# Bias products of an attention block as rows instead of columns, and the preparation of the MLP weights one slot earlier

## The chip, the cores and the metric

The kernel runs on one core of a Trainium2 chip. The metric is the device time of one execution in microseconds. TensorE does the matrix products, VectorE, ScalarE and GpSimd (POOL) the elementwise work, and SyncE (SP) issues all DMAs. TensorE's clock has two levels, 1.2 and 2.4 GHz; the profile gives the granted one as 0.50 and 1.00.

## The reference, cut to what matters

One block of cross attention with an MLP, for 16 batches of 256 queries and 256 tokens, width 512, 16 heads of 32, hidden width 2048:

```
q, kv = ln(x) * g_q + b_q, ln(ctx) * g_kv + b_kv
qp, kp, vp = q @ Wq.T + bq, kv @ Wk.T + bk, kv @ Wv.T + bv
scores = qp . kp / sqrt(32) - scale * dist + offset      # per head
x = x + softmax(scores) @ vp @ Wo.T + bo
h = gelu((ln(x) * g_m + b_m) @ W1.T + b1)
out = x + h @ W2.T + b2
```

The layer norms' shifts b_q, b_kv and b_m are not added to the activations. As (y * g + b) @ W.T is y @ (g * W).T + b @ W.T, the gains go into the weights and the products b @ W.T (the "shifts' products") into the biases. The change is about those products.

## The kernel before, in words

All large products are f16 in three passes (high by high, high by low, low by high), so each weight is split once into a rounded high part and the rest. Before that it is scaled by the inverse of a norm: ScalarE squares the staged f32 weight and sums over its rows, VectorE adds up, TensorE sums over partitions (`total`), VectorE copies the sum and works out the square of the norm (`square_norm`), GpSimd takes the root (`norm_root`), VectorE forms the factor (`gains`), ScalarE writes the high part (`weight_hi`, `w1_hi`, `w2_hi`) and VectorE the low part (`weight_lo`, `w1_lo`, `w2_lo`). W1 and W2 are staged in 8 chunks of 4 pieces (128x512) in a ring of three chunks. W2's split pieces are stored to DRAM (`store_w2`), since only three fit on the chip, and are loaded again for every batch (`load_w2`).

Each engine has its own program, an order written out by hand over the same slots, from -32 to 297. One slot is one item: one head of one batch. In slot s TensorE computes the scores of item s+1 (`scores`, one bank of PSUM, so it waits until VectorE has read the scores before), VectorE takes the maximum of item s (`score_max`, line 1054), ScalarE the exponentials (`exps`, line 773), and so on down the pipeline. Projections of queries and keys come every four slots, those of values and outputs every sixteen. `mlp_up` starts in slot 31 and `mlp_down` in slot 37 (`DOWN`); from there each slot holds one step of each. Slots -32 to -1 prepare the attention weights, slots 1 to 35 those of the MLP, beside the attention's first items. Within an engine all runs in order, so a waiting instruction holds everything behind it.

`weight_bias`, `value_bias` and `w1_bias` make the shifts' products: the weight's 128x128 f32 block is the loaded operand, one column of `cols` the moving one, so the result is a column of 128. There are 16 such products for each of W_k, W_q, W_v and each chunk of W1; each appears as two records of `128x1 f32`. `bias_column`, `bias_v_spread` and `bias1_columns` read the columns from PSUM. `value_bias_out` (line 541) multiplies W_v's bias, spread over a tile, by W_o. `warm` (line 653) and `keep_busy` (line 659) are fillers: products whose result nobody reads. `keep_busy` runs in slots 7 to 36 and fills each slot to 16 units of one 512 column product.

Of the kernel before, what the change touches and what calls it, by code (L numbers as in the profile page):

```python
# [13 lines left out]
P = 128  # L14
# [37 lines left out]
def build_block(nc, x, ctx, tok_xy, q_xy, mask, w_qkv, w_o, w_1, w_2, cols, b_o, b_2, sp_scale, sp_offset, out, w2_dram):  # L52
# [16 lines left out]
    with es:  # L69
# [80 lines left out]
        sq = sb("sq", [P, LC, T], F32, at["x1_n"])  # L150
        bias_v = sb("bias_v", [P, KT, P], F32, at["x1"] + KT * D * 4)
# [51 lines left out]
        s_mkept, s_tv, s_brow, s_bcol, s_brow_o, s_bo_all = sem("s_mkept"), sem("s_tv"), sem("s_brow"), sem("s_bcol"), sem("s_brow_o"), sem("s_bo_all")  # L203

# [18 lines left out]
        TOTAL = (-30, -28, -4, 0) + tuple(range(1, 33, 4))  # L223
        NORM = (-28, -25, -3, 0) + tuple(range(2, 34, 4))
        GAIN = (-27, -24, -3, 1) + tuple(range(3, 35, 4))
# [122 lines left out]
        def sync_program(engine):  # L348
# [49 lines left out]
            def load_residual(t):  # L398
                ring = t % X1_RING
                gate.wait_ge(s_wsq, WSQ[3])  # L400
                gate.wait_ge(s_brow_o, 1)
                gate.wait_ge(s_mkept, DMA)
                gate.wait_ge(s_colsum, 1)
                gate.wait_ge(s_store[ring], DMA * (t // X1_RING))
                e.dma_start(x1[:, ring, :], x_rows[t]).then_inc(s_res[ring], DMA)
# [43 lines left out]
            for slot in range(FIRST_SLOT, LAST_SLOT + 1):  # L449
# [42 lines left out]
                for step in due(slot, -5, ITEM, 2 * N_CHUNKS * KT):  # L492
# [5 lines left out]
        def tensor_program(engine):  # L498
            e, gate = engine, Gate(engine)

            def weight_bias(sec, quarters):
# [3 lines left out]
                for k in quarters:  # L505
                    gate.wait_ge((s_wk if sec == SEC_K else s_wq)[k], DMA)
                    for m in range(KT):

                        col = sec * KT + m
                        mm = e.matmul(ps_bias[sec][:, col:col + 1], w_stage[sec][:, k, m * P:(m + 1) * P],  # L510
                                      cols_sb[:, b_ln + k:b_ln + k + 1], start=((k, m) == (0, 0)), stop=((k, m) == (KT - 1, KT - 1)))
                if KT - 1 in quarters:
                    mm.then_inc(s_brow)

            def value_bias(m):
                sec, b_ln = SEC_V, B_KV
                gate.wait_ge(s_w[0], DMA)
                gate.wait_ge(s_cols, DMA)
                gate.wait_ge(s_bcol, BIAS_Q)
                col = sec * KT + m  # L520
                for k in range(KT):
                    mm = e.matmul(ps_bias[sec][:, col:col + 1], w_stage[sec][:, k, m * P:(m + 1) * P],
                                  cols_sb[:, b_ln + k:b_ln + k + 1], start=(k == 0), stop=(k == KT - 1))
                if m == KT - 1:
                    mm.then_inc(s_brow)

            def w1_bias(c, m):
                col = c * CH + m
                for k in range(KT):
                    gate.wait_ge(s_wc[c % C_STAGES][k], n_staged(c))  # L530
                    mm = e.matmul(ps_bias_1[:, col:col + 1], staged(c, k)[:, m * P:(m + 1) * P],
                                  cols_sb[:, B_M + k:B_M + k + 1], start=(k == 0), stop=(k == KT - 1))
                if m == CH - 1:
# [114 lines left out]

            def warm(count):
# [15 lines left out]
            for slot in range(FIRST_SLOT, LAST_SLOT + 1):  # L665
                for at_slot, count in ((-32, 10), (-30, 3), (-8, 10), (-6, 8), (-3, 2), (-2, 8)):
# [42 lines left out]
        def scalar_program(engine):  # L709
# [72 lines left out]
            def dist_square(b, c):  # L782
# [4 lines left out]
                gate.wait_ge(s_hlo, 2 * (b - 2))  # L787
# [583 lines left out]
```

## Time and profile before

| | us |
|---|---|
| median of 3 runs (1252.31 to 1252.36) | 1252.32 |
| the profiled execution | 1252.47 |
| its span, first to last instruction | 1250.6 |
| TensorE busy | 1220.2 |
| VectorE busy | 993.6 |
| GpSimd busy | 992.0 |
| ScalarE busy | 851.3 |
| mean granted clock of TensorE | 0.986 |

Busy times are of the span, whatever the stage. A group of instructions is named by line, engine, operation and tiles (out, then in). In the order of time several equal instructions are merged, with their count behind an x. The idle time in brackets is the engine's own before the instruction, with the one that ended it.

### The profile page before, as it was taken

How to read it: one execution, taken by the hardware profiler on the slowest of the kernel's cores; microseconds unless marked ns; L12 is line 12 of the kernel's file. 1: busy time of each engine (PE TensorE's matmuls, PEld its weight loads, DVE VectorE, ACT ScalarE, POOL GpSimd, SP SyncE). 2: the span in 40 equal slices, each digit the busy share in tenths (PEclk: the TensorE clock that was granted, in tenths of full speed). 3: DMA queues.
4: the chain of work that ended last, by engine and by line, in shares of the span. 5: the costliest groups of instructions: out<-in, count | busy, mean ns of one | idle time of the engine just before them, and what ended most of it. 6: DMA issues, size and time to landing. Idle time of an engine off the chain costs nothing.

```text
span 1250.6 us, 27744 instructions
## 1 busy us (share of the span) xinstructions
PE 1220.2 (98%) x9424; PEld 819.0 (65%) x9424; DVE 993.6 (79%) x2656; ACT 851.3 (68%) x1914; POOL 992.0 (79%) x1286
## 2 busy tenths in 40 slices
PE   9888988999999999999999999999999999999998
PEld 6656455666667666666666676666666666666664
DVE  5799998888878888888888989888888787778321
ACT  5867757676877677676767677776767677676331
POOL 5478897989898898989898998989898987767320
PEclk9788999999999999999999999999999999999999
DMA  6699999888999898998999998998889897879543
GB/s 185 197 188 208 224 224 195 192 189 209 209 194 222 180 214 198 193 203 201 198 205 218 180 223 182 202 203 203 194 206 208 195 208 176 173 170 180 142 113 123
DMA packets 468686, 241.69 MB, mean 193 GB/s; under 512 B 384048, under 2 KB 408896, under 8 KB 468544
## 3 DMA queue, kind: packets, MB, share of 16 engines
q1 hardware_dynamic: 468544, 239.91, 85.6%
q8 instruction: 75, 1.23, 0.4%
q14 instruction: 67, 0.55, 0.1%
HBM read 109.66 MB, written 12.58 MB: 98 GB/s over the span
## 4 chain that ended last, share of the span: by engine, by line
PE 86%; DVE 8%; issue 2%; ACT 1%; POOL 1%; DMA 1%; SPq 0%; POOLq 0%; DVEq 0%; ACTq 0%
PE ps_up L630 26%; PE ps_down L645 26%; PE ps_qk L566 12%; PE ps_vo L590 6%; PE ps_vo L587 6%; PE ps_s L601 5%; PE ps_pv L615 4%; DVE p_nat L1071 1%; DVE soft L1054 1%; PE ps_down L510 1%; DVE w L999 1%; DVE w L1005 1%; DVE x_nat L1031 1%; PE ps_down L541 0%; DVE qk_parts L1045 0%
## 5 line engine op out<-in xcount | busy, mean ns | idle before, releaser
L1248 POOL TENSOR_SCALAR p_nat<-soft,row_inv 128x256 f16<-128x256 f32 x512 | 332.1, 658 | 61.2 <-DVE row_inv L1065 59.4
L630 PE MATMUL ps_up<-hT,w 128*128 128x256 f16 x3072 | 377.2, 273 | 3.1 <-ACT u L805 2.7
L645 PE MATMUL ps_down<-w,hid 128*128 128x512 f16 x1536 | 372.9, 379 | 0.8 <-DVE hid L1103 0.4
L630 PEld LDWEIGHTS ps_up<-hT,w 128*128 128x128 f16 x3072 | 300.3, 98 | 93.2 <-ACT u L805 3.2
L773 ACT ACTIVATE soft<-soft,neg_max 128x256 f32<-128x256 f32 x512 | 255.2, 500 | 117.2 <-DVE neg_max L1054 116.2
L1054 DVE CUSTOM_DVE_ANT_0 soft<-ps_s,soft,factor 128x256 f32<-128x256 f32 x512 | 225.4, 476 | 116.7 <-PE ps_s L601 115.9
L1071 DVE SCALAR_TENSOR_TENSOR p_nat<-soft,row_inv,p_nat 128x256 f16<-128x256 f32 x512 | 297.6, 620 | 2.1 <-POOL p_nat L1248 1.9
L1256 POOL TENSOR_SCALAR soft<-dist,scale_neg,offset 128x512 f32<-128x512 f32 x256 | 244.3, 954 | 14.0 <-DVE p_nat L1071 13.6
L645 PEld LDWEIGHTS ps_down<-w,hid 128*128 128x128 f16 x1536 | 148.6, 97 | 132.4 <-DMA w<-x_scratch 1.4
L805 ACT ACTIVATE u<-ps_up,bias,up_scale 128x256 f32<-128x256 f32 x256 | 142.3, 556 | 124.9 <-PE ps_up L630 121.5
L1264 POOL TENSOR_SCALAR hid<-u,hid_scale 128x1024 f16<-128x1024 f32 x64 | 77.3, 1208 | 105.0 <-ACT u L811 105.0
L766 ACT ACTIVATE qk_parts<-ps_qk,bias_qkv 128x512 f16<-128x512 f32 x128 | 86.9, 679 | 100.1 <-DMA stack<-stack 83.3
L1103 DVE SCALAR_TENSOR_TENSOR hid<-u,hid_scale,hid 128x1024 f16<-128x1024 f32 x64 | 98.0, 1531 | 47.9 <-POOL hid L1264 47.9
L601 PE MATMUL ps_s<-stack 97*128 97x256 f16 x512 | 100.6, 278 | 17.4 <-DVE neg_max L1054 17.0
L566 PE MATMUL ps_qk<-xT,w_q 128*128 128x256 f16 x768 | 99.2, 281 | 2.6 <-DVE qk_parts L1045 2.6
L566 PE MATMUL ps_qk<-xT,w_k 128*128 128x256 f16 x768 | 96.2, 276 | 0.7 <-DVE qk_parts L1045 0.7
L773 ACT ACTIVATION_READ_ACCUMULATOR soft<-soft,neg_max 128x1 f32 x512 | 96.5, 188 | 0.0
L587 PE MATMUL ps_vo<-w_v,xT 128*128 128x512 f16 x384 | 95.8, 387 | 0.0
L590 PE MATMUL ps_vo<-w_o,attnT 128*128 128x512 f16 x384 | 93.3, 379 | 0.0
L566 PEld LDWEIGHTS ps_qk<-xT,w_q 128*128 128x128 f16 x768 | 77.2, 101 | 14.2 <-issue 1.7
L566 PEld LDWEIGHTS ps_qk<-xT,w_k 128*128 128x128 f16 x768 | 76.1, 99 | 11.7 <-DVE qk_parts L1045 1.4
L601 PEld LDWEIGHTS ps_s<-stack 97*128 97x128 f16 x512 | 44.5, 99 | 58.3 <-issue 28.3
(122 smaller groups left out, 1569.5 us busy)
## 6 DMA issues: line engine op xcount, KB each, us to landing
w<-x_scratch SPq DMA_DIRECT2D x256, 256.0 KB, 3.1
stack<-qk_parts SPq DMA_DIRECT2D x256, 96.0 KB
raw<-in_ctx SPq DMA_DIRECT2D x32, 256.0 KB, 3.4
raw<-in_x SPq DMA_DIRECT2D x32, 256.0 KB, 3.1
c_stage<-in_w SPq DMA_DIRECT2D x32, 256.0 KB, 3.6
x<-in_x SPq DMA_DIRECT2D x32, 256.0 KB, 3.5
out<-x SPq DMA_DIRECT2D x32, 256.0 KB, 3.2
tok_rows<-in_tok_xy SPq DMA_DIRECT2D x16, 256.0 KB, 4.4
```

The source lines that it names most:

```text
L566: mm = e.matmul(ps_qk[:, which * L:(which + 1) * L], w_sec[sec][:, wp, k, hg * P:(hg + 1) * P], xT_of(b, which)[:, :, xp * KT + k, :], sta ...
L587: mm = e.matmul(ps_vo[:], xT_of(b, 0)[:, tt, xp * KT + k, :], w_sec[SEC_V][:, wp, k, :], start=first, stop=last)
L590: mm = e.matmul(ps_vo[:], attnT[:, b % 2, xp, k, tt * P:(tt + 1) * P], w_sec[SEC_O][:, wp, k, :], start=first, stop=last)
L601: mm = e.matmul(ps_s[:, lc * T:(lc + 1) * T], stack[0:97, ring, j, 0, lc * P:(lc + 1) * P], stack[0:97, ring, j, 1, :], start=True, stop=True)
L630: mm = e.matmul(ps_up[s % 2][:, 0:L], w_1_sb[:, wp, k, m * P:(m + 1) * P], hT[:, b % 2, :, xp * KT + k, :], start=(k, wp, xp) == (0, 0, 0) ...
L645: mm = e.matmul(ps_down[tt][:], hid[:, chunk % HID_RING, i, hp, tt * P:(tt + 1) * P], w_2_sb[:, s % W2_RING, wp, :], start=(m == 0 and (hp ...
L773: e.activation(soft[:, ring, lc, :], soft[:, ring, lc, :], ACT.Exp, scale=-1.0, bias=neg_max[:, ring, lc:lc + 1], accum_out=row_sum[:, rin ...
L805: e.activation(u[:, chunk % U_RING, i, :], ps_up[s % 2][:, 0:L], ACT.Identity, scale=up_scale[:, chunk % N_CHUNKS:chunk % N_CHUNKS + 1], b ...
L1054: e.tensor_tensor_reduce(soft[:, ring, lc, :], ps_s[:, lc * T:(lc + 1) * T], soft[:, ring, lc, :], factor[:, 0:1], 3.0e38, ALU.add, ALU.mi ...
L1071: mine = e.scalar_tensor_tensor(out=p_nat[:, nat, LO, lc, :], in0=soft[:, ring, lc, :], scalar=row_inv[:, ring, lc:lc + 1], in1=p_nat[:, n ...
L1248: mine = e.tensor_scalar(p_nat[:, nat, HI, lc, :], soft[:, ring, lc, :], row_inv[:, ring, lc:lc + 1], 1.0, ALU.mult, ALU.mult)
L1256: e.tensor_scalar(soft[:, i % SOFT_RING, :, :], dist[:, b % DIST_RING, :, :], scale_neg[:, h:h + 1], offset_sb[:, h:h + 1], ALU.mult, ALU. ...
```

## The change

The shift's column becomes the loaded operand (one column) and the weight the moving one, 512 f32 columns at a time, read in the order "every 128th column first". The result is one row, in which four values of one partition lie side by side. ScalarE copies the row to on-chip memory (`bias_row`, `bias_rows_1`) and a DMA on SP's queue turns it into columns (`bias_turn`, `bias_turn_1`); W1's four rows lie on partitions 0, 32, 64 and 96 of one bank, which a filler product clears first (`clear_rows`). The squares of distances wait for the turned row of W_q, whose place they use. W_v's product moves from slots -2, 0 and 2 to slot -3. Chunk loads, squares, totals, gains, roundings and stores of W1 and W2 move one slot ahead, and with them the hidden norm; W2's piece 0 is loaded in slot 35 instead of 36, the others as before. `keep_busy` starts in slot 0 instead of 7, into another bank up to slot 8, and counts a product of W1 as 4 units instead of 8. The fillers ahead of the first slots are regrouped.

```diff
-        TOTAL = (-30, -28, -4, 0) + tuple(range(1, 33, 4))
-        NORM = (-28, -25, -3, 0) + tuple(range(2, 34, 4))
-        GAIN = (-27, -24, -3, 1) + tuple(range(3, 35, 4))
+        TOTAL = (-30, -28, -4, 0) + tuple(range(0, 32, 4))
+        NORM = (-28, -25, -3, 0) + tuple(range(1, 33, 4))
+        GAIN = (-27, -24, -3, 1) + tuple(range(2, 34, 4))
...
+            def bias_turn(sec):
+                gate.wait_ge(s_row, AT[sec] + 1)
+                e.dma_start(bias_qkv[:, sec * KT:(sec + 1) * KT], (row_q if sec == SEC_Q else row_kv)[:]).then_inc(s_rowd[sec], DMA)
+
+            def bias_turn_1():
+                gate.wait_ge(s_row, ROW_1)
+                for c in range(N_CHUNKS):
+                    e.dma_start(bias_1[:, c * CH:(c + 1) * CH], rows_1[32 * c:32 * c + 1, :]).then_inc(s_rowd_1, DMA)
...
+                for sec, at_slot in ((SEC_K, -25), (SEC_Q, -24), (SEC_V, -1)):
+                    if slot == at_slot:
+                        bias_turn(sec)
+                if slot == 18:
+                    bias_turn_1()
...
-                for s in due(slot, 21, ITEM, MT):
+                for s in due(slot, 20, ITEM, MT):
                     store_w2(s)
-                if slot == DOWN - 1:
-                    load_w2(0)
-                for s in due(slot, DOWN - 1, ITEM, N_STEPS - 1):
-                    load_w2(s + 1)
+                for s in due(slot, DOWN - 2, ITEM, N_STEPS):
+                    load_w2(s)
...
-                for step in due(slot, -5, ITEM, 2 * N_CHUNKS * KT):
+                for step in due(slot, -6, ITEM, 2 * N_CHUNKS * KT):
                     load_chunk(*divmod(step, KT))
...
+            def by_column(w):
+                return w.rearrange("p (m q) -> p q m", m=KT)
...
                 for k in range(KT):
-                    mm = e.matmul(ps_bias[sec][:, col:col + 1], w_stage[sec][:, k, m * P:(m + 1) * P],
-                                  cols_sb[:, b_ln + k:b_ln + k + 1], start=(k == 0), stop=(k == KT - 1))
...
+                    mm = e.matmul(ps_bias[sec][0:1, :], cols_sb[:, b_ln + k:b_ln + k + 1], by_column(w_stage[sec][:, k, :]),
+                                  start=(k == 0), stop=(k == KT - 1))
+                mm.then_inc(s_brow)
+
+            def w1_bias(c, k):
+                gate.wait_ge(s_wc[c % C_STAGES][k], n_staged(c))
+                mm = e.matmul(ps_bias_1[32 * c:32 * c + 1, :], cols_sb[:, B_M + k:B_M + k + 1], by_column(staged(c, k)),
+                              start=(k == 0), stop=(k == KT - 1))
...
-                for at_slot, count in ((-32, 10), (-30, 3), (-8, 10), (-6, 8), (-3, 2), (-2, 8)):
+                for at_slot, count in ((-32, 10), (-30, 1), (-28, 1), (-8, 12), (-6, 6)):
...
-                for sec, quarters, at_slot in ((SEC_K, range(3), -31), (SEC_K, range(3, KT), -29), (SEC_Q, range(1), -29),
-                                              (SEC_Q, range(1, 3), -28), (SEC_Q, range(3, KT), -27)):
+                for sec, at_slot in ((SEC_K, -31), (SEC_Q, -29), (SEC_V, -3)):
                     if slot == at_slot:
-                        weight_bias(sec, quarters)
-                for m, at_slot in enumerate((-2, 0, 2, 2)):
-                    if slot == at_slot:
-                        value_bias(m)
+                        weight_bias(sec)
+                if slot == 0:
+                    clear_rows()
...
-                if 7 <= slot < DOWN:
+                if 0 <= slot < DOWN:
                     taken = 1 + (3 if due(slot, 9, GROUP, N_HG) else 0) + (6 if slot % 2 else 0) + (6 if slot >= UP else 0)
-                    taken += vo_done + (8 if due(slot, 1, ITEM, MT) else 0)
-                    keep_busy(max(0, SLOT_STEPS - taken))
+                    taken += vo_done + (4 if due(slot, 1, ITEM, MT) else 0)
+                    taken += 16 if slot == 4 else 0
+                    keep_busy(ps_pv if slot < 9 else ps_down[0], max(0, SLOT_STEPS - taken))
...
+            def bias_row(sec):
+                gate.wait_ge(s_brow, AT[sec] + 1)
+                if sec == SEC_V:
+                    gate.wait_ge(s_rowd[SEC_K], DMA)
+                e.activation((row_q if sec == SEC_Q else row_kv)[:], ps_bias[sec][0:1, :], ACT.Copy).then_inc(s_row)
@@ dist_square
                 gate.wait_ge(s_hlo, 2 * (b - 2))
+                gate.wait_ge(s_rowd[SEC_Q], DMA)
...
+                for sec, at_slot in ((SEC_K, -26), (SEC_Q, -24), (SEC_V, -2)):
+                    if slot == at_slot:
+                        bias_row(sec)
+                if slot == 17:
+                    bias_rows_1()
...
-                for step in due(slot, -3, ITEM, 2 * N_CHUNKS * KT):
+                for step in due(slot, -4, ITEM, 2 * N_CHUNKS * KT):
                     chunk_square(*divmod(step, KT))
-                for step in due(slot, 3, ITEM, MT):
+                for step in due(slot, 2, ITEM, MT):
                     w1_hi(*divmod(step, KT))
-                for s in due(slot, 19, ITEM, MT):
+                for s in due(slot, 18, ITEM, MT):
                     w2_hi(s)
...
-                for n in due(slot, 1, KT, 2 * N_CHUNKS):
+                for n in due(slot, 0, KT, 2 * N_CHUNKS):
                     weight_sums(AT_W1 + n)
...
-                for step in due(slot, 4, ITEM, MT):
+                for step in due(slot, 3, ITEM, MT):
                     w1_lo(*divmod(step, KT))
-                for s in due(slot, 20, ITEM, MT):
+                for s in due(slot, 19, ITEM, MT):
                     w2_lo(s)
```

## Rows read from the trace of the kernel before

**Rows 1.** The page: the chain that ended last, by engine.

```profile
PE 86%; DVE 8%; issue 2%; ACT 1%; POOL 1%; DMA 1%; SPq 0%; POOLq 0%; DVEq 0%; ACTq 0%
```

**Rows 2.** Busy time of PE, PEld, DVE, ACT, POOL; PEclk; last row line 1054 alone.

```profile
39.80:49.50 9.70, 9.48 (x52) 7.04 (x52) 5.40 (x21) 9.49 (x23) 2.82 (x4) 0.65 0.69 212
78.40:115.60 37.20, 30.30 (x232) 22.44 (x232) 36.48 (x112) 29.68 (x79) 30.96 (x42) 0.87 0.97 227
115.60:198.00 82.40, 75.47 (x553) 44.42 (x552) 77.44 (x232) 55.90 (x146) 68.58 (x92) 0.98 0.93 212
210.00:1145.00 935.00, 934.99 (x7522) 632.93 (x7520) 783.23 (x2083) 671.32 (x1500) 811.68 (x1047) 1.00 0.91 198
...
78.40:115.60 37.20, 7.96 (x36) 0.87 0.97 227
```

**Rows 3.** The same columns, for stretches of one clock.

```profile
41.10:47.90 6.80, 6.80 (x29) 4.58 (x28) 3.12 (x14) 6.59 (x19) 2.82 (x4) 0.50 0.68 204
51.40:54.80 3.40, 2.61 (x25) 2.53 (x23) 3.26 (x11) 2.28 (x5) 2.40 (x5) 1.00 0.87 318
54.80:65.00 10.20, 9.30 (x30) 5.82 (x31) 9.96 (x33) 5.95 (x18) 9.71 (x15) 0.50 0.36 85
```

**Rows 4.** TensorE in order of time, 0 to 20 us.

```profile
1.52 4.45 PE L653 MATMUL ps_pv<-attnT 128*128 128x512 f16 x10 [1.52 <-POOL attnT L1283]
6.17 5.25 PE L510 MATMUL ps_down<-cols,w_stage 128*128 128x1 f32 x24 [0.21 <-DMA w_stage<-in_w_qkv]
12.81 6.96 PE L510 MATMUL ps_down<-cols,w_stage 128*128 128x1 f32 x32
19.63 0.57 PE L552 MATMUL ps_up<-sums,one 128*128 128x2 f32 x2
```

**Rows 5.** TensorE in order of time, three places.

```profile
51.28 1.84 PE L522 MATMUL ps_down<-cols,w_stage 128*128 128x1 f32 x16
...
60.59 5.80 PE L541 MATMUL ps_down<-w_stage,bias_v 128*128 128x512 f32 x8
...
189.70 2.10 PE L659 MATMUL ps_down<-w_k 128*128 128x512 f16 x9
```

**Rows 6.** VectorE in order of time: the copies of W_q's and W_o's totals.

```profile
20.24 0.16 DVE L889 COPY tot<-ps_up 128x2 f32<-128x2 f32 x1 [2.98 <-PE ps_up L552]
...
44.14 0.16 DVE L889 COPY tot<-ps_up 128x1 f32<-128x1 f32 x1 [3.37 <-PE ps_up L552]
```

**Rows 7.** ScalarE in order of time, 24 to 52 us.

```profile
24.64 2.56 ACT L740 ACTIVATE w_q<-w_stage,gain 128x512 f16<-128x512 f32 x4 [5.12 <-DVE factor L919]
...
35.70 2.56 ACT L740 ACTIVATE w_v<-w_stage,gain 128x512 f16<-128x512 f32 x4 [0.41 <-DVE gain L913]
38.17 0.58 ACT L734 ACTIVATE ps_down<-c_stage 128x512 f32<-128x512 f32 x1
...
51.26 0.60 ACT L757 ACTIVATE v_parts<-ps_vo 128x512 f16<-128x512 f32 x1
```

**Rows 8.** Waits, 38 to 210 us: total, times, longest.

```profile
PE ps_s L601 <- DVE neg_max L1054: 17.0, 15, 2.8
DVE row_one L1062 <- ACT soft L773: 3.6, 1, 3.6
DVE b_o L979 <- PE ps_down L541: 1.2, 1, 1.2
DVE v_parts L1040 <- ACT v_parts L757: 0.9, 2, 0.7
```

**Rows 9.** ScalarE and TensorE in order of time, at the first gelu.

```profile
194.54 0.72 ACT L752 ACTIVATE w<-c_stage,w_scale 128x512 f16<-128x512 f32 x1 [1.64 <-DMA x_scratch<-w]
...
202.49 1.48 PE L630 MATMUL ps_up<-hT,w 128*128 128x256 f16 x12 [2.75 <-ACT u L805]
```

**Rows 10.** DMA issues up to 230 us: size, us from issue to landing.

```profile
stack<-mask_row SPq DMA_DIRECT2D x1, 8.0 KB, 2.3
...
q_neg<-in_q_xy SPq DMA_DIRECT2D x1, 32.0 KB, 5.0
```

More of the change, by code:

```diff
@@ L401, in load_residual @@
                 gate.wait_ge(s_brow_o, 1)
-                gate.wait_ge(s_mkept, DMA)
-                gate.wait_ge(s_colsum, 1)
+                if t >= KT:
+                    gate.wait_ge(s_rowd_1, N_CHUNKS * DMA)
                 gate.wait_ge(s_store[ring], DMA * (t // X1_RING))
@@ L499, in tensor_program, with weight_bias @@
             e, gate = engine, Gate(engine)
-            def weight_bias(sec, quarters):
+            def by_column(w):
+                return w.rearrange("p (m q) -> p q m", m=KT)
+            def weight_bias(sec):
                 gate.wait_ge(s_cols, DMA)
                 b_ln = B_Q if sec == SEC_Q else B_KV
[L505 to L509, printed above, removed]
-                        mm = e.matmul(ps_bias[sec][:, col:col + 1], w_stage[sec][:, k, m * P:(m + 1) * P],
-                                      cols_sb[:, b_ln + k:b_ln + k + 1], start=((k, m) == (0, 0)), stop=((k, m) == (KT - 1, KT - 1)))
-                if KT - 1 in quarters:
-                    mm.then_inc(s_brow)
@@ L527, in w1_bias @@
[L527 to L533, printed above, removed]
+                if sec == SEC_V:
+                    gate.wait_ge(s_row, ROW_K)
+                for k in range(KT):
+                    if sec == SEC_V:
+                        gate.wait_ge(s_w[0], DMA)
+                    else:
+                        gate.wait_ge((s_wk if sec == SEC_K else s_wq)[k], DMA)
+                    mm = e.matmul(ps_bias[sec][0:1, :], cols_sb[:, b_ln + k:b_ln + k + 1], by_column(w_stage[sec][:, k, :]),
+                                  start=(k == 0), stop=(k == KT - 1))
@@ L647, in mlp_down, with clear_rows @@
                 mm.then_inc(s_m2)
+            def clear_rows():
+                e.matmul(ps_bias_1[:], w_sec[SEC_K][:, HI, 0, 0:P], w_sec[SEC_K][:, HI, 0, :], start=True, stop=True)
             def warm(count):
@@ L653, in warm, with keep_busy @@
                     e.matmul(ps_pv[:], fill[:, 0, 0:P], fill, start=True, stop=True)
-            def keep_busy(count):
-                gate.wait_ge(s_bo_all, 1)
+            def keep_busy(bank, count):
+                if bank is ps_down[0]:
+                    gate.wait_ge(s_bo_all, 1)
+                gate.wait_ge(s_wlo, AT[SEC_K] + 1)
                 for _ in range(count):
-                    e.matmul(ps_down[0][:], w_sec[SEC_K][:, HI, 0, 0:P], w_sec[SEC_K][:, HI, 0, :], start=True, stop=True)
+                    e.matmul(bank[:], w_sec[SEC_K][:, HI, 0, 0:P], w_sec[SEC_K][:, HI, 0, :], start=True, stop=True)
             STEPS = KT * len(PASSES)
@@ L960, in bias_column @@
                 part = slice(sec * KT, (sec + 1) * KT)
-                gate.wait_ge(s_brow, AT[sec] + 1)
-                e.tensor_tensor(bias_qkv[:, part], ps_bias[sec][:, part], cols_sb[:, B_IN + sec * KT:B_IN + (sec + 1) * KT], ALU.add).then_inc(s_bcol)
+                gate.wait_ge(s_rowd[sec], DMA)
+                e.tensor_tensor(bias_qkv[:, part], bias_qkv[:, part], cols_sb[:, B_IN + sec * KT:B_IN + (sec + 1) * KT], ALU.add).then_inc(s_bcol)
                 gate.wait_ge(s_bcol, 2 * AT[sec] + 1)
@@ L967, in bias_v_spread @@
             def bias_v_spread():
-                gate.wait_ge(s_brow, AT[SEC_V] + 1)
+                gate.wait_ge(s_rowd[SEC_V], DMA)
                 gate.wait_ge(s_wsq, WSQ[3])
                 part = slice(SEC_V * KT, (SEC_V + 1) * KT)
-                e.tensor_tensor(bias_qkv[:, part], ps_bias[SEC_V][:, part], cols_sb[:, B_IN + SEC_V * KT:B_IN + (SEC_V + 1) * KT],
+                e.tensor_tensor(bias_qkv[:, part], bias_qkv[:, part], cols_sb[:, B_IN + SEC_V * KT:B_IN + (SEC_V + 1) * KT],
                                 ALU.add).then_inc(s_tv)
@@ L1133, in vector_program @@
                         gains(w)
-                if slot == 32:
+                if slot == 31:
                     hidden_norm()
-                if slot == 34:
+                if slot == 33:
                     hidden_scales()
@@ L1149, in vector_program @@
                     bias_out()
-                if slot == 19:
+                if slot == 21:
                     bias1_columns()
@@ L1290, in gpsimd_program @@
                         norm_root(w)
-                if slot == 33:
+                if slot == 32:
                     norm_root(N_W)
```

27 lines of the change are left out of this document (15 added, 12 removed).

## The prediction

> **What bounds the kernel now.** I read the chain of waits first, then the table of stretches, then the clock, then the order of time in the first 210 us. The chain gives 86% to TensorE [rows 1]. The table by stage says more. From 210 to 1145 us TensorE is busy 934.99 of 935 us at full clock [rows 2]; nothing of the change issues there (W2's loads for steps 1 and up keep their slots), so that stage is a constant, and only the moment at which it begins can move. Before it the bound is another. From 78.4 to 115.6 us VectorE is busy 36.48 of 37.20 us for 9 items (line 1054 has 36 records there, four per item), so 4.13 us an item; from 115.6 to 198 it is 77.44 of 82.40. TensorE has 30.30 and 75.47 there [rows 2], and in 38 to 210 us it waits 17.0 us, 15 times, for VectorE to read the score bank [rows 8]. From 39.8 to 49.5 us it is ScalarE, busy 9.49 of 9.70 us, where VectorE has 5.40 [rows 2]. Before that nothing is full: one chain of small results runs from W_q's products to W_v's rounding.
>
> The clock is low in places, and not where TensorE rests. Between 51.4 and 54.8 us TensorE is busy 2.61 of 3.40 us, nearly all of it 128x1 products, and the next 10.2 us are granted 0.50, which is 1.2 GHz; so are 41.1 to 47.9 us, after another set of them [rows 3, 5]. The page of the skill that bears on it says otherwise (below).
>
> **The change, part by part.** My unit is the profiled execution, 1252.47 us (span 1250.6 and 1.87 around it); the median of the runs is 0.15 lower.
>
> *Products of W_k and W_q.* Before: 16 products each of 128 columns loaded for one moved. 32 records took 6.96 us [rows 4], so 16 products take 7.0 us at 1.2 GHz. W_k's run from 6.17 us, and W_q's total stands at 19.63 us behind 56 records, 5.25 + 6.96 us [rows 4]. After: 4 products each with 512 f32 columns moved. The one group of that size took 5.80 us for 4, part of it at 0.50 [rows 3, 5]; its records are pairs, so each product is four passes over 512 columns. A pass is about 0.21 us at 2.4 GHz (nine f16 ones end in 2.10 us, the last 0.38 included) and 0.43 us at 1.2 GHz (ten in 4.45 us) [rows 4, 5]. So 0.86 or 1.71 us a product, 3.4 or 6.8 us a matrix. If the clock rises once wide columns stream without a pause, W_k's products end between 10 and 12 us, W_q's total would be free at 14 to 16 us, and ScalarE's sums of squares and VectorE's first W_k rounding, ahead of it on their queues, hold it near 16. VectorE waited 2.98 us for this total [rows 6], and behind it ScalarE 5.12 us for W_q's factor [rows 7]; all work up to W_v's gain at 35.7 us hangs on it. That is 3.6 us at most by this one wait, and I take 3.0, since W_q's row must now turn before ScalarE may square the distances. That wait is new: row copy 0.6 us, then a small DMA. The nearest landings are 2.3 us (mask row) and 5.0 us (coordinates) [rows 10]; at 2.3 it ends inside ScalarE's idle 5.12 us, at 5.0 it gives back about 2 us. On SP's queue nothing is due behind it but the turns of the query tiles, which are not ready. If the clock stays low, 2 x 6.8 us and three small groups end at 20.9: 1.3 later than now. Bounds -4.5 and +1.3; I take **-3.0**.
>
> *W_v's product, in slot -3.* It leaves slots -2 to 2 (four times eight records, of which sixteen take 1.84 us at full clock; [rows 5]) and puts 3.4 us, or 6.8 cold, ahead of the second key projection. TensorE had fillers and idle time there, and the copy of its row stands behind ScalarE's own queue. 0; at 6.8 us the first scores come late by up to 3, still before ScalarE takes them up.
>
> *ScalarE before the first exponentials.* This is what the change costs. The squares of a W1 chunk move one slot ahead, so one more stands in front (0.58 us, and 0.2 as my estimate for the read of its sum), and the copy of W_v's row is new, 128x512 before for about 0.60 us [rows 7]; its bounds are 0.25 and 0.67, 0.60 is the nearest row. The other copies fall into idle time. From W_v's rounding at 35.70 us to 50 us ScalarE has no room [rows 2, 7]: 1.4 us. Worse, W1's first total now stands in slot 0 beside W_o's: VectorE sums chunk 0 before it takes W_o's total, and TensorE's queue (value projection, next scores) stands behind W1's total. Today VectorE waits 3.37 us for W_o's total until 44.14 [rows 6]; TensorE would free it some 1.5 us sooner, without eight narrow records at half clock, but ScalarE gives the square later, so nothing is won, and about 0.5 is lost. **+1.9**, bounds +0.6 and +3.
>
> *Slots 0 to 17.* A W1 step is one product of 0.86 us where eight records take 0.95 (16 in 1.84; [rows 5]). By the formula fillers go from 167 to 239: 36 in slots 0 to 6, and up to 4 more (0.86 us) in each of slots 7 to 16. A slot is then filled to about 16 x 0.215 = 3.5 to 3.8 us, under VectorE's 4.13. So fillers cost 0 while the clock is full, and keep it there. What full clock buys is only what VectorE waited for: 1.2 us for the spread bias product (four products, 3.4 instead of 5.80) and about 0.7 for a value tile [rows 5, 8]. The rest of the half-clock time (17 us in [rows 3], more behind the means of 0.87 and 0.98 in [rows 2]) lies beside VectorE's work. **-1.9**.
>
> *Slots 31 to 37.* ScalarE's last W2 rounding waits 1.64 us for its store to land and takes 0.72, then come three table loads and the first gelu; VectorE waits 3.6 us for the exponentials behind them and TensorE 2.75 us [rows 8, 9]. With the rounding a slot ahead its wait and its length leave: **-2.3**. VectorE's last rounding leaves too. The load of W2's step 0 moves to slot 35 with its wait on the same store, so SP stands still there as it did in slot 36; 0.
>
> Sum: -3.0 + 1.9 - 1.9 - 2.3 = -5.3; 1252.47 - 5.3 = 1247.2, less 0.15: **1247.0**.
>
> **Two rules of the skill.** The Trainium skill, "TensorE: Matmul & The Clock Gate", section "Why this matters for your kernels", ties the clock to idle gaps between bursts. The stretch 51.4 to 54.8 us [rows 3] does not agree: it was busy and lost the clock. By that rule the faster products could hurt, since TensorE would stand idle some 4 us before the first query projection; the price is the cold W_v product above.
>
> The Trainium skill, "Advanced Engine Details and Errata", section "Memory Cachelines", says that a penalty falls due when each access goes to another 16-byte line. The new products move every 128th column in turn, so each element is on another line. No row here shows such a read; what it would do is the first rival.
>
> **Rivals.** *A: the strided read halves the rate.* Then a wide product takes 1.71 us at any clock. For: W1's stage is read in steps of 512 bytes, all matmuls of the trace read runs of 128 or more. Against: an f32 element has four passes' time. W_q's total comes +1.3, ScalarE's +1.9 stays, a W1 slot holds 3.6 + 0.86 = 4.45 us against VectorE's 4.13, +0.3 x 16 = +5, and -4.2 from the last two parts: +4.0, **1256.3**. It decides from a product of about 1.4 us. *B: a product with a single loaded column does not lift the clock*, so the start stays at 1.2 GHz. For: the first ten f16 fillers did not lift it, as the records behind them take 0.22 us each against 0.115 at full clock [rows 4, 5]. +1.3 + 1.9 - 4.2 = -1.0, **1251.3**. *C: the change does not do what it says at slots 33 to 37*: SP's queue, not the slot number, sets when stores land, so ScalarE waits as before: -3.0, **1249.3**. *D: more is hung on the clock than I see*, TensorE's 17 us of waits shift to real progress: another -5, **1242**.
>
> **How the numbers follow.** My forecast 0.49; B 0.18, A 0.14, C 0.12, D 0.07. A measurement of this kernel can tell 0.2%, 2.5 us, from no change. Faster: 0.9 of the forecast, D, half of C, a little of B: 0.60. Slower: A and a tail of the forecast, where the turn takes 5 us and ScalarE's +3 comes: 0.16. Same: 0.24. The range goes from D's 1241.5 to 1254.5, which leaves out most of A.
>
> **What would show it.** Products on the new line: 0.86 us apart, or 1.71. The clock at 1.00 from before 20 us to the end; any 0.50 behind 55 us speaks against the fillers' part. W_q's total near 16 instead of 19.63. W_v's rounding on ScalarE about 3 us sooner than 35.70, and W_o's total at VectorE only about 1 us sooner than 44.14. VectorE's wait for the spread product gone. No ScalarE wait on the store ahead of the first gelu, TensorE's 2.75 us wait shortened. From then on TensorE as full as before, from some 5 us earlier. The prediction is wrong if this last stage changes, or if VectorE's items in slots 7 to 16 take more than 4.2 us.

## The result: slower, not faster

| kernel | median us (range, runs) | ratio to before, 95% interval | profiled: time / span, us |
|---|---|---|---|
| before | 1252.34 (1252.31 to 1255.13, 4) | 1 | 1252.47 / 1250.6 |
| changed | 1260.80 (1259.82 to 1262.26, 4) | 1.0063 [1.0045, 1.0081] | 1259.82 / 1258.0 |

The forecast was 1247.0; the change costs 8.5 us by the medians and 7.4 by the two spans. The starts of the score pairs on TensorE cut the span into parts (slot n begins with the scores of item n):

| us | to scores(0) | slots 0 to 17 | 18 to 35 | 36 and 37 | rest | span |
|---|---|---|---|---|---|---|
| before | 38.3 | 79.6 | 77.3 | 12.1 | 1043.3 | 1250.6 |
| changed | 43.3 | 85.2 | 77.3 | 9.5 | 1042.7 | 1258.0 |
| difference | +5.0 | +5.6 | 0 | -2.6 | -0.6 | +7.4 |

Two places lose, the gelu's place gains what was forecast, and the long stage is as full as in [rows 2]. First the start. TensorE in order of time (start, us, instruction, in brackets the idle time before it and its releaser) answers to [rows 4]:

```profile
1.52 4.45 PE L668 MATMUL ps_pv<-attnT 128*128 128x512 f16 x10 [1.52 <-POOL attnT L1317]
6.07 7.12 PE L535 MATMUL ps_down<-w_stage,cols 128*1 128x512 f32 x8
13.57 7.12 PE L535 MATMUL ps_down<-w_stage,cols 128*1 128x512 f32 x8
20.84 0.28 PE L563 MATMUL ps_up<-sums,one 128*128 128x2 f32 x2
20.98 2.75 PE L668 MATMUL ps_pv<-attnT 128*128 128x512 f16 x12
...
32.11 2.72 PE L577 MATMUL ps_qk<-xT,w_q 128*128 128x256 f16 x12 [5.26 <-DVE qk_parts L1079]
...
34.98 7.12 PE L535 MATMUL ps_down<-w_stage,cols 128*1 128x512 f32 x8
42.03 1.48 PE L577 MATMUL ps_qk<-xT,w_k 128*128 128x256 f16 x12
43.35 0.39 PE L612 MATMUL ps_s<-stack 97*128 97x256 f16 x2
```

Four wide products (eight records) take 7.12 us, the tail of the last included, so 1.78 us a product and not 0.86 (start to start it is 1.74). W_q's total stands at 20.84 us, 1.2 later than the 19.63 of [rows 4]. W_v's product, which I had put at no cost, stands bare between the first query projection and the second key projection, and the first scores wait behind it.

The second place is slots 7 to 16. The stretch (columns as in [rows 2]: length, busy time with count of PE, PEld, DVE, ACT, POOL, then PEclk, DMA share, GB/s) of ten slots in the changed kernel:

```profile
78.20:123.90 45.70, 45.70 (x228) 17.19 (x227) 41.76 (x122) 34.03 (x90) 34.87 (x47) 1.00 0.93 200
```

and the same ten slots before:

```profile
72.10:113.00 40.90, 31.99 (x245) 23.56 (x242) 40.18 (x122) 32.01 (x84) 33.13 (x44) 0.87 1.00 223
```

VectorE was the full engine (40.18 of 40.90). Now TensorE is: 45.70 of 45.70, at full clock. The bound has moved to an engine for which I had forecast at most 3.8 us a slot; a slot now takes 4.57 us instead of 4.09, which is 4.8 of the 5.6 us lost there. One slot of it:

```profile
82.98 1.47 PE L577 MATMUL ps_qk<-xT,w_q 128*128 128x256 f16 x12
84.39 1.90 PE L542 MATMUL ps_up<-c_stage,cols 128*1 128x512 f32 x2
86.22 1.25 PE L676 MATMUL ps_pv<-w_k 128*128 128x512 f16 x5
87.30 0.38 PE L612 MATMUL ps_s<-stack 97*128 97x256 f16 x2
```

The W1 product stands there for 1.90 us (its two records, the end of the last included), and 1.25 us of fillers behind it is work that nobody needs.

The third place gained. The waits of 38 to 218 us (us in total, times, longest) answer to [rows 8], and the first gelu product to [rows 9]:

```profile
DVE row_one L1096 <- ACT soft L801: 1.6, 1, 1.6
```
```profile
210.56 1.49 PE L641 MATMUL ps_up<-hT,w 128*128 128x256 f16 x12 [0.20 <-ACT u L834]
```

VectorE's wait fell from 3.6 to 1.6 us, TensorE's from 2.75 to 0.20, and slots 36 and 37 from 12.1 to 9.5 us. The store's wait is gone from ScalarE's queue, though another stands a little ahead of it:

```profile
200.46 0.69 ACT L794 ACTIVATE qk_parts<-ps_qk,bias_qkv 128x512 f16<-128x512 f32 x1 [3.40 <-DMA stack<-stack]
```

### The profile page after: what moved, and what is told of

Its sections match the earlier page's. It is cut to its first block, busy times and chain, and to the rows that moved or that the text cites. A ratio compares the mean times of both kernels' runs of the same rounds, so it can differ in the third digit from the quotient of the medians.

```text
span 1258.0 us, 27547 instructions
## 1 busy us (share of the span) xinstructions
PE 1237.2 (98%) x9318; PEld 788.2 (63%) x9318; DVE 979.3 (78%) x2656; ACT 853.6 (68%) x1918; POOL 997.5 (79%) x1286
## 4 chain that ended last, share of the span: by engine, by line
PE 91%; DVE 5%; ACT 2%; issue 1%; DMA 1%; POOL 0%; SPq 0%; POOLq 0%; DVEq 0%; ACTq 0%
PE ps_up L641 26%; PE ps_down L656 26%; PE ps_qk L577 12%; PE ps_vo L601 6%; PE ps_vo L598 6%; PE ps_s L612 5%; PE ps_pv L626 4%; PE ps_up L542 2%; PE ps_down L535 2%; PE ps_down L676 1%; DVE p_nat L1105 1%; DVE soft L1088 1%; DVE w L1039 1%; PE ps_pv L676 1%; PE ps_pv L668 0%
## 5 line engine op out<-in xcount | busy, mean ns | idle before, releaser
L1282 POOL TENSOR_SCALAR p_nat<-soft,row_inv 128x256 f16<-128x256 f32 x512 | 327.8, 650 | 60.8 <-DVE row_inv L1099 60.0
L1105 DVE SCALAR_TENSOR_TENSOR p_nat<-soft,row_inv,p_nat 128x256 f16<-128x256 f32 x512 | 288.6, 603 | 1.0 <-POOL p_nat L1282 0.8
L1290 POOL TENSOR_SCALAR soft<-dist,scale_neg,offset 128x512 f32<-128x512 f32 x256 | 250.5, 979 | 14.6 <-DVE p_nat L1105 12.6
L1298 POOL TENSOR_SCALAR hid<-u,hid_scale 128x1024 f16<-128x1024 f32 x64 | 80.0, 1250 | 102.6 <-ACT u L840 102.6
L1137 DVE SCALAR_TENSOR_TENSOR hid<-u,hid_scale,hid 128x1024 f16<-128x1024 f32 x64 | 92.7, 1448 | 47.9 <-POOL hid L1298 47.9
```

Of the source, the lines that this page charges most:

```text
L1105: mine = e.scalar_tensor_tensor(out=p_nat[:, nat, LO, lc, :], in0=soft[:, ring, lc, :], scalar=row_inv[:, ring, lc:lc + 1], in1=p_nat[:, n ...
L1282: mine = e.tensor_scalar(p_nat[:, nat, HI, lc, :], soft[:, ring, lc, :], row_inv[:, ring, lc:lc + 1], 1.0, ALU.mult, ALU.mult)
L1290: e.tensor_scalar(soft[:, i % SOFT_RING, :, :], dist[:, b % DIST_RING, :, :], scale_neg[:, h:h + 1], offset_sb[:, h:h + 1], ALU.mult, ALU. ...
```

## The experiments

The theory after the result: the strided read of the moved operand doubles the price of a wide product (rival A of the prediction), and this alone turns a gain into a loss; the rest of the change does about what was forecast. Rivals: the row form itself (copies, turns, a single loaded column), the added fillers, or the shift by one slot. Each time is a median, with its ratio to the kernel before on the same chip.

**e1: the same products over contiguous columns.** The row then comes out in another order, and ScalarE's copy puts it right.

```diff
 def by_column(w):
-    return w.rearrange("p (m q) -> p q m", m=KT)
+    return w
...
-e.activation(row[:], ps_bias[sec][0:1, :], ACT.Copy)
+e.activation(row[:].rearrange("o (q m) -> o q m", m=KT),
+             ps_bias[sec][0:1, :].rearrange("o (m q) -> o q m", m=KT), ACT.Copy)
```

> The changed kernel, but the shifts' products read the weight's 512 columns in their order; the reordering is done by ScalarE when it copies the row. Theory S (the strided read halves the rate of the moved operand): the eight records of a matrix, 7.12 us apart from first to last end in the changed kernel, shrink to about 3.6 us; slots 7 to 16 go from 4.55 to 3.7 to 4.1 us on TensorE, the first scores come 5 us or more sooner than 43.35 us, and the time falls by 8 to 13 us, to 1247 to 1253. Theory C (an f32 product with a single loaded column runs at this rate however it reads): the records stay 0.88 us apart and the time stays within 1 us of 1260.8.

1248.25 (1246.48 to 1248.87), ratio 0.9964 [0.9949, 0.9979]: 12.5 us less than the changed kernel, and faster than before. All records of the line in the changed kernel, then in e1 (ns, min/median/max):

```profile
L535 PE MATMUL ps_down<-w_stage,cols x24: 1027/1047/1049, 6.1 to 41.0; 128*1 128x512 f32 x24
```
```profile
L535 PE MATMUL ps_down<-w_stage,cols x24: 589/592/592, 6.8 to 33.0; 128*1 128x512 f32 x24
```

And TensorE of e1 in order of time:

```profile
6.79 3.59 PE L535 MATMUL ps_down<-w_stage,cols 128*1 128x512 f32 x8 [0.82 <-DMA w_stage<-in_w_qkv]
10.76 3.59 PE L535 MATMUL ps_down<-w_stage,cols 128*1 128x512 f32 x8
14.71 0.35 PE L563 MATMUL ps_up<-sums,one 128*128 128x2 f32 x2
...
27.17 2.72 PE L577 MATMUL ps_qk<-xT,w_q 128*128 128x256 f16 x12 [5.13 <-DVE qk_parts L1079]
29.97 3.59 PE L535 MATMUL ps_down<-w_stage,cols 128*1 128x512 f32 x8
33.50 1.48 PE L577 MATMUL ps_qk<-xT,w_k 128*128 128x256 f16 x12
36.51 0.39 PE L612 MATMUL ps_s<-stack 97*128 97x256 f16 x2 [1.53 <-DMA stack<-stack]
```

Four products take 3.59 us, 0.90 each with the tail of the last, and start 0.86 apart as forecast. W_q's total stands at 14.71 and the first scores at 36.51 where the changed kernel has 43.35. In slots 7 to 16 TensorE is no longer full:

```profile
68.20:110.20 42.00, 37.89 (x227) 16.70 (x227) 40.55 (x124) 32.31 (x88) 33.25 (x45) 1.00 1.06 227
```

**e2: the changed kernel with the fillers of before.**

```diff
-if 0 <= slot < DOWN:
+if 7 <= slot < DOWN:
...
-taken += vo_done + (4 if due(slot, 1, ITEM, MT) else 0)
+taken += vo_done + (8 if due(slot, 1, ITEM, MT) else 0)
```

> The changed kernel with the fillers of before: from slot 7, a product of W1 counted as 8 units; the strided read stays. Theory F (in slots 7 to 16 the fillers, on top of products that take 1.75 us, make TensorE the bound): TensorE's slots 7 to 16 go from 4.55 to about 3.7 to 4.3 us, VectorE becomes full again, the time falls by 3 to 5 us to about 1256.5. Theory P (the whole loss is made before the first scores): no change beyond 1 us. If the clock falls to 0.50 in slots 0 to 16 again, the time may even rise.

1256.13 (1254.57 to 1257.66), 1.0037 [1.0024, 1.0049]: 4.7 less than the changed kernel. The fillers, put at nothing in the forecast, cost this while the strided product fills the slot. Slots 0 to 17 fell from 85.2 to 79.0 us; of that 1.5 was lost again in slots 18 to 35 (78.8 for 77.3) and 1.6 in the rest.

**e3: the kernel before, with only the numbers of the slots moved** (preparation one slot ahead, W2's loads two; column products and fillers as they were).

> The kernel before with nothing but the preparation of W1 and W2 one slot ahead (totals in even slots, W2's piece 0 loaded in slot 35); products as columns and fillers as before. My account: ScalarE and W1's first total cost 1.3 us before the first exponentials, the gelu's stretch gives back 2.3 us: 1251.3, range 1249 to 1253. Rival: the stretch at slots 33 to 37 is set by SP's queue and gives nothing back: 1253.6.

1253.16 (1251.86 to 1256.23), 1.0011 [1.0000, 1.0023]: just outside my own range, if anything slower than before, and near the rival's figure, though not for the rival's reason. Slots 36 and 37 take 9.1 us instead of 12.1, so the gain at the gelu is there, but slots 0 to 35 take 161.1 instead of 157.0. Part of the store's wait goes over to the turn of a key tile, ScalarE at 190 us:

```profile
190.16 0.69 ACT L764 ACTIVATE qk_parts<-ps_qk,bias_qkv 128x512 f16<-128x512 f32 x1 [1.97 <-DMA stack<-stack]
```

This trace also shows how far one profiled execution can be trusted at its start. Up to its first scores TensorE runs the same program as before, yet it is 2.4 us sooner at W_q's total (17.18 us for 19.63) and at the first scores (35.83 for 38.27):

```profile
6.39 2.91 PE L508 MATMUL ps_down<-cols,w_stage 128*128 128x1 f32 x24 [0.42 <-DMA w_stage<-in_w_qkv]
...
17.18 0.56 PE L550 MATMUL ps_up<-sums,one 128*128 128x2 f32 x2
...
35.83 0.39 PE L599 MATMUL ps_s<-stack 97*128 97x256 f16 x2 [0.35 <-DMA stack<-stack]
```

The 24 narrow records take 2.91 us here and 5.25 in [rows 4]: here the clock rose beside them, and fell again with TensorE never idle (columns as in [rows 2]):

```profile
6.60:10.00 3.40, 3.40 (x28) 2.81 (x28) 1.09 (x4) 2.44 (x8) 3.00 (x6) 1.00 1.02 376
10.02:23.60 13.58, 13.58 (x55) 10.82 (x56) 9.64 (x31) 8.35 (x19) 9.36 (x12) 0.50 0.78 189
```

So the start of one profiled execution of a column kernel holds some 2.4 us of chance, and a comparison with it is no better than that.

**e4: e1 with the slots of before** (contiguous rows, no shift).

> Rows with contiguous reads and the new fillers, but the preparation of W1 and W2 in its old slots. Theory S with the parts additive: the difference to the kernel with both (e1) is that of the shift alone (e3 to before), -1 us for the shift, so 1248 to 1254, about 1 us above e1. Rival: the shift hurts once VectorE and ScalarE are the bound in the first slots, then this kernel is the faster of the two by 1 us or more.

1248.17 (1247.33 to 1249.55), 0.9972 [0.9959, 0.9984]: 0.1 from e1. The shift is worth nothing in either form; the rows over contiguous columns make the whole gain. The store's wait ahead of the gelu is gone here without the shift, behind 3.22 us for a key tile's turn; W2's rounding follows at once:

```profile
191.06 0.73 ACT L782 ACTIVATE w<-c_stage,w_scale 128x512 f16<-128x512 f32 x1
```

Where the time lies in the profiled executions:

| us | to scores(0) | slots 0 to 35 | 36 and 37 | rest | span |
|---|---|---|---|---|---|
| before | 38.3 | 157.0 | 12.1 | 1043.3 | 1250.6 |
| e3, columns, shift | 35.8 | 161.1 | 9.1 | 1044.2 | 1250.2 |
| e4, contiguous rows | 36.1 | 157.4 | 10.6 | 1043.2 | 1247.3 |
| e1, contiguous rows, shift | 36.5 | 158.0 | 9.7 | 1042.7 | 1247.0 |

**e5: e1 with e2's edit** (contiguous rows, old fillers).

> Contiguous products and the shift (e1) with the fillers of before (from slot 7, 8 units for a product of W1). In the changed kernel taking the new fillers away was worth about 5 us, on top of products of 1.75 us. If it was the sum of both that made TensorE the bound, then here, with products of 0.88 us, the new fillers cost at most the 0.5 to 1 us that the first scores of slots 1 to 4 stand behind them: 1247.3 to 1248.3 against 1248.25. If the fillers alone are the cost, 1243 to 1245. If they hold the clock up and this matters, slower than e1 by 1 us or more, with 0.50 in the profile between slots 0 and 16.

1247.96 (1247.21 to 1249.16), 0.9962 [0.9948, 0.9975]: 0.3 from e1. The same fillers that cost 4.7 us beside strided products cost nothing beside contiguous ones.

**e6: e5, with W_q's row in a buffer of its own place and the wait for its turn moved from ScalarE's distances to POOL's bias tile.**

```diff
-row_q = sb("row_q", [1, D], F32, at["x1_n"])
+row_q = sb("row_q", [1, D], F32, at["soft"])
...
-gate.wait_ge(s_rowd[SEC_Q], DMA)     # ScalarE, ahead of the distances
+gate.wait_ge(s_rowd[SEC_Q], DMA)     # POOL, ahead of the bias tile
```

> e5 with W_q's row in another place of memory, so that the squares of the distances no longer wait for its turn (in e1 ScalarE stood 3.21 us for that DMA and rounded W_q from 22.24 us). W_q's rounding on ScalarE starts near 20.7 us, 1.5 us sooner. If ScalarE is on the chain there, the first scores come 1 to 1.5 us sooner and so does the end; if VectorE is (its masks end at 23.87 us and its own W_q rounding follows at once), 0 to 0.5 us.

1248.72 (1248.09 to 1250.48), 0.9973 [0.9960, 0.9985]: no gain over e5 (1247.96), a miss. In e1 ScalarE waits for the turn and takes W_q's rounding up at 22.24 us:

```profile
20.63 0.91 ACT L820 ACTIVATE dist<-tok_rows,q_neg 128x256 f32<-128x256 f32 x2 [3.21 <-DMA bias_qkv<-row_q]
22.24 2.54 ACT L768 ACTIVATE w_q<-w_stage,gain 128x512 f16<-128x512 f32 x4
```

In e6 it does so at 20.23 us, and yet TensorE's first query projection stands only 0.4 us sooner than in e1, and 0.1 sooner than in e5 (26.88), its twin but for this edit:

```profile
20.23 2.56 ACT L768 ACTIVATE w_q<-w_stage,gain 128x512 f16<-128x512 f32 x4 [1.72 <-DVE factor L952]
```
```profile
26.75 2.72 PE L577 MATMUL ps_qk<-xT,w_q 128*128 128x256 f16 x12 [5.23 <-DVE qk_parts L1078]
```

The turn takes 3.2 us of ScalarE's time, but VectorE's splitting of the query tile is what ends last. (The profiled execution of e6 is the slowest of its ten.)

**e7: e6 with 22 more fillers in TensorE's idle gap ahead of that projection.**

```diff
-for at_slot, count in ((-32, 10), (-30, 1), (-28, 1), (-8, 12), (-6, 6)):
+for at_slot, count in ((-32, 10), (-30, 1), (-28, 1), (-8, 12), (-6, 28)):
```

> e6 with 22 more fillers ahead of the first query projection, where TensorE stood idle 5.13 us in e1 and the clock then fell to 0.50. Expected: no 0.50 near 26 to 30 us, the first query projection in 1.47 us instead of 2.72, the first scores and the end 1.2 us sooner than e6. If the fillers run longer than the gap, part of that is lost; if the chain goes through VectorE alone, 0.

1247.52 (1246.46 to 1248.94), 0.9960 [0.9946, 0.9973], 1.2 less than e6:

```profile
19.95 6.21 PE L668 MATMUL ps_pv<-attnT 128*128 128x512 f16 x28
26.63 1.47 PE L577 MATMUL ps_qk<-xT,w_q 128*128 128x256 f16 x12 [0.47 <-DMA xT<-x_nat]
...
35.10 0.39 PE L612 MATMUL ps_s<-stack 97*128 97x256 f16 x2 [1.95 <-DMA stack<-stack]
```

The projection starts when it did but takes 1.47 us instead of 2.72, and the first scores come 0.7 us sooner than in e6. The next query projection, at 38.01 us, still runs at half rate (2.74 us), as in e6.

**e8, e9, e11: e1 with the strided read back at one of its three places** (W_v's product; W1's; W_k's and W_q's), **and e10: e9 with the fillers of before.**

```diff
-by_column(staged(c, k))                               # e9 and e10; e8 and e11 alike at line 535
+staged(c, k).rearrange("p (m q) -> p q m", m=KT)
```

> e1 with only W_v's product strided again, so 7.1 instead of 3.6 us on TensorE ahead of the second key projection. The prediction put this product at 0. In e1 TensorE waits 1.53 us for a DMA before the first scores, so of 3.5 us more 2 us should reach them: first scores 38.5 instead of 36.51 us. If ScalarE takes them up no sooner anyway, the end is the same as e1's within 0.5 us; if the loss is passed on, the end is 2 us later, about 1250.2.

> e1 (contiguous products, the shift, the new fillers) with only W1's products strided again. The first scores stay at e1's 36.5 us. If a strided product and the new fillers together make TensorE the bound, its slots 7 to 16 take 4.55 us again and the end is 4 to 5 us later than e1: 1252.2 to 1253.3 against 1248.25. If the whole loss of the changed kernel lies before the first scores, the end is within 1 us of e1's.

> e9 with the fillers of before. With contiguous products the fillers made no difference (1248.25 new, 1247.96 old). If the two costs only bite together, this kernel is within 1 us of those, 1247.5 to 1249; if the strided W1 product costs by itself, 2 us or more above them.

> e1 with only the products of W_k and W_q strided. They take 7.1 us each instead of 3.6, so W_q's total comes near 20.8 instead of 14.71 us. If the chain through W_q's total sets the first scores, they come about 5 us later, at 41.5 us, and the end with them: 1252.5 to 1253.5. If it is taken up later, less. With V's share (e8, +1.5) and W1's (e9) the sum should be the 12.5 us between e1 and the changed kernel; what is missing in the sum is an overlap.

| kernel | median us | ratio to before | over its contiguous twin |
|---|---|---|---|
| e8, W_v strided | 1249.71 | 0.9978 [0.9967, 0.9989] | +1.5 (e1) |
| e9, W1 strided | 1253.59 | 1.0013 [1.0003, 1.0024] | +5.3 (e1) |
| e10, the same, old fillers | 1249.14 | 0.9975 [0.9964, 0.9985] | +1.2 (e5) |
| e11, W_k and W_q strided | 1254.09 | 1.0012 [1.0003, 1.0022] | +5.8 (e1) |

TensorE in e8, then in e11:

```profile
29.69 7.12 PE L535 MATMUL ps_down<-w_stage,cols 128*1 128x512 f32 x8
36.74 1.48 PE L577 MATMUL ps_qk<-xT,w_k 128*128 128x256 f16 x12
```
```profile
13.80 7.12 PE L535 MATMUL ps_down<-w_stage,cols 128*1 128x512 f32 x8
21.08 0.28 PE L563 MATMUL ps_up<-sums,one 128*128 128x2 f32 x2
...
41.55 0.39 PE L612 MATMUL ps_s<-stack 97*128 97x256 f16 x2
```

The differences are between medians from different chips, on which the kernel before had 1251.74 (e1) to 1252.33 (e9 to e11); the intervals of e8 and e1 overlap, so the 1.5 is the least sure of them. The traces agree with it: e8's first scores come 1.6 us later than e1's (38.1 for 36.5), e11's 5.0 later (41.55 for 36.51). The ten slots 7 to 16 in e9, then in e10:

```profile
72.40:118.10 45.70, 45.70 (x227) 17.19 (x226) 41.43 (x122) 34.05 (x90) 35.21 (x48) 1.00 0.90 198
```
```profile
70.10:110.50 40.40, 38.42 (x184) 13.41 (x182) 38.25 (x116) 31.92 (x84) 32.25 (x43) 0.96 1.04 220
```

e9 has the 45.70 us of the changed kernel to the digit, all of it TensorE's; without the fillers the strided product still has room. So for W1 most of the loss needs both, a product of 1.78 us and fillers counted as if it were 0.86; the stride alone costs 1.2, a little more than the 1 us of the expectation:

| median us | old fillers | new fillers |
|---|---|---|
| W1 contiguous | 1247.96 (e5) | 1248.25 (e1) |
| W1 strided | 1249.14 (e10) | 1253.59 (e9) |

**e12: the changed kernel once more,** on the same chip as e11.

> The changed kernel once more, beside the three above, for the sum: 1259.8 to 1262.3, ratio to before 1.0045 to 1.008.

1260.67 (1260.43 to 1261.87), 1.0071 [1.0055, 1.0088]. The three strided places add up to 1.5 + 5.3 + 5.8 = 12.6 us over e1; the changed kernel measures 12.4 over it. That they meet so closely is in part luck, as the medians of the kernel before alone differ by 0.6 us between these chips.

## Why the prediction was wrong, step by step

**The step that failed** is the price of a wide product: "So 0.86 or 1.71 us a product", with the first taken. It is 1.78 us here at full clock, because of the stride; contiguous it is 0.90. I had taken it for a question of clock, and the clock answered as hoped. The PEclk column can't show that, since it reads 1.00 from the start in both kernels. The durations do: the ten f16 passes at 1.52 us take 4.45 us in both; the ten at 21.77 us before still took 4.43, while twelve at 20.98 us in the changed kernel take 2.75, and e1's first wide products, at 6.79 us, are already at 3.59 for four. So rival B is false. But half of this is luck: it was not the wide products that lifted the clock. It rises early in every execution read but that of before, and not at a fixed moment: the ten fillers from 1.52 us take 4.45 us in most of them, but 4.19 in e5 and 3.65 in e9, where the rise falls among them, ahead of any wide product; in e3 it came beside column products. What the wide products did is keep it, where the narrow ones lost it again at 10.0 us (e3).

```profile
1.52 3.65 PE L668 MATMUL ps_pv<-attnT 128*128 128x512 f16 x10 [1.52 <-POOL attnT L1317]
```

The change is slower by rival A. It costs in each place where the prediction used the 0.86:

- *W_k and W_q*, -3.0: measured +1.2 at W_q's total, the upper bound that I named (+1.3). Over contiguous products it costs 5.8 us (e11). With contiguous ones the total came 4.9 us sooner than in the profile of before, of which 1.8 was left at the first scores (below). But that profile starts 2.4 us late by chance, and beside e3's first scores at 35.83 nothing is left (e1 36.51, e4 36.09). So neither e1 nor e4 shows the 3.0 at the first scores.
- *W_v*, "0": wrong in the strided form (+1.5, e8). I had seen that the second key projection stands behind it, and that first scores up to 3 us late might follow; what failed is "still before ScalarE takes them up". The 1.6 us at e8's first scores came through to the end.
- *Fillers*, "cost 0 while the clock is full": right for contiguous products (e1 against e5, 0.3) and wrong by 4.5 to 4.7 us for strided ones (e9 against e10; e2 against the changed kernel). The filling formula counts the product as four passes; at twice their price a slot comes to 4.57 us, above VectorE's 4.1. My "3.5 to 3.8 us" rested on the 0.86.
- *ScalarE before the exponentials*, +1.9: there, and about the right size. The start of slot 36 comes 1.6 us later in e3 than before, and 1.0 later in e1 than in e4 (sums of the table at e4). *Slots 31 to 37*, -2.3: 2.6 in the changed kernel and 3.0 in e3, but beside rows the shift gives 0.9 of it only (9.7 in e1 for 10.6 in e4), since the store's wait goes without it. In the end the shift is +1.4 beside column products (e3; the interval has 0 to +2.9) and 0.1 beside rows (e1 against e4). Totals in slot 0 show as waits on VectorE, for ScalarE's late square, and again on its rounding:

```profile
48.05 0.16 DVE L915 TENSOR_REDUCE sums<-ssq 128x1 f32<-128x4 f32 x1 [2.50 <-ACT ps_down L750]
...
53.24 1.42 DVE L1023 SCALAR_TENSOR_TENSOR w_o<-w_stage,factor,w_o 128x512 f16<-128x512 f32 x2 [1.49 <-ACT w_o L768]
```

- *Full clock in slots 0 to 17*, -1.9: it came (0.87 to 1.00 over the ten slots) and brought nothing that lasts. e1 takes 77.7 us there for 79.6 before, but 80.4 for 77.3 in slots 18 to 35, so 158.0 for 157.0 over both; and e5, without the new fillers, is as fast as e1. What takes the time back in slots 18 to 35 no run shows.

Rival A had the mechanism and a price 4.5 us too low (1256.3 for 1260.8): W_q's +1.3 was right, but W_v's product was left out, a slot came to 4.57 and not 4.45, and the -1.9 for the full clock stood in it too. I gave it 0.14 though nothing in the trace of before spoke for full rate under a stride; "four passes' time" for an element was an argument and no row. Rivals C and D are not seen: the gelu's wait went, and full clock won nothing further. With the stride taken out the sum was near, 1247.0 forecast and 1248.25 measured (e1), or -5.3 against -3.5 on e1's chip; but its parts were not, as the last three points show, so some of that is luck.

The products' doubled time agrees with the Trainium skill, "Advanced Engine Details and Errata", section "Memory Cachelines", which sets a penalty on reads that go to another 16-byte line each time; this case adds its size at full clock, 7.12 us for 3.59. The other rule that I weighed (the Trainium skill, "TensorE: Matmul & The Clock Gate", section "Why this matters for your kernels": idle gaps cost the clock) holds in one place here, against my doubt: after 5.26 us of idle time the stretch is granted 0.50,

```profile
26.80:30.00 3.20, 0.05 (x1) 0.00 (x0) 3.13 (x7) 2.95 (x5) 0.59 (x1) 1.00 0.63 60
30.00:36.80 6.80, 4.69 (x17) 2.44 (x18) 3.54 (x14) 1.96 (x4) 0.00 (x0) 0.50 0.89 286
36.80:43.30 6.50, 6.50 (x19) 1.55 (x17) 3.51 (x6) 5.38 (x10) 3.00 (x3) 1.00 0.59 142
```

and with the gap filled (e7) it isn't:

```profile
26.60:35.10 8.50, 6.53 (x34) 3.08 (x34) 2.55 (x11) 4.62 (x8) 1.74 (x3) 1.00 0.85 267
```

(In e7 the 0.50 comes later instead, from 37.8 to 41.1 us, after 1.95 and 2.51 us of idle time around the first scores.) The rule does not cover [rows 3], where the clock fell with TensorE busy 2.61 of 3.40 us, nor e3, where it fell with TensorE busy 3.40 of 3.40, 24 of the 28 records narrow ones.

Seven versions are faster than the kernel before (e1, e4 to e8, e10). The quickest are e7 (1247.52), e5 (1247.96), e4 (1248.17) and e1 (1248.25), 0.28% to 0.40% under it; their intervals overlap, and these runs don't separate them. The changed kernel would be mended by e1's edit alone.

Why do the 4.9 us won at W_q's total shrink to 1.8 at the first scores? In the kernel before the two projections stand at

```profile
31.16 1.47 PE L566 MATMUL ps_qk<-xT,w_q 128*128 128x256 f16 x12 [1.25 <-DVE qk_parts L1045]
...
33.93 1.48 PE L566 MATMUL ps_qk<-xT,w_k 128*128 128x256 f16 x12 [0.73 <-DVE qk_parts L1045]
```

At the query projection e1 (27.17 us) is still 4.0 ahead. At the second key projection (33.50) it is 0.4 ahead: the query projection takes 2.72 us at the half clock, and W_v's product with its 3.59 us now stands between the two. From there to the first scores e1 needs 3.0 us and the kernel before 4.3, since its fillers and its own W_v products come behind the key projection. What is left open: what takes back the gain of slots 0 to 17 in slots 18 to 35; and why the clock rises when it does, as early as the fillers (e9) or only in the first wide product (e7, whose first eight records take 4.08 us for 3.59), and in the profiled execution of before not until about 27 us, where fillers first run at full rate (28.02 us).

## What to carry to other kernels

When operands are swapped so that a matrix is moved instead of loaded, look at how the moved side is read: keep the wide read contiguous and put the reordering on the small result; here that version was the faster by 12.5 us in all. (Only f32 at a step of 512 bytes was run.) A filler that is free under one bound is not free under the next: recount the slot with the measured price of what is new in it. And where a sum has a factor of two with no row to decide it, the case with the doubled price needs more than a seventh of the chance, above all when it multiplies three terms.

## What the runs showed of the hardware

- A product with one loaded and 512 moved f32 columns takes 0.90 us contiguous and 1.78 us at a step of 512 bytes, at full clock, both with the tail of the last; its records grow from 592 to 1047 ns.
- At the half clock the stride costs nothing more. W_v's contiguous product in e11 and the strided one in the changed kernel both start while the granted clock is 0.50 (up to 38.2 us in e11, 36.8 in the changed kernel), with records 0.86 and 0.87 us apart. The strided one takes 7.12 us across that change of clock, and 7.12 us at full clock (13.57 us).

```profile
35.20 3.38 PE L535 MATMUL ps_down<-w_stage,cols 128*1 128x512 f32 x4
```

- Products with one loaded and 512 wide moved columns keep the full clock: twelve fillers behind the eight of W_k and W_q take 2.75 us. Behind products with 128 loaded columns and one moved it fell to 0.50 though TensorE had been busy 3.40 of 3.40 us (e3).
- Ahead of its first change the granted clock reads 1.00, also where durations are at half rate: ten f16 passes in 4.43 us at 21.77 us before, and 4.45 at 1.52 us in most kernels. At the head of a trace durations are the better witness.
- The turn of one 2 KB row inside the chip lands 2.0 us (changed kernel, e11, e12) to 3.3 us (e5) behind its issue, and keeps ScalarE waiting 2.1 to 3.4 us.
